# Linear-attention kernel on one core: the order of work in the entry, on four engines

## The reference

```python
xn = _layernorm(x)
def layer(h, p):                        # 8 layers, scan
    q = elu(h @ wq + bq) + 1; k = elu(h @ wk + bk) + 1; v = h @ wv + bv
    kv = einsum('bshd,bshm->bhdm', k, v)
    z = 1 / (einsum('bshd,bhd->bsh', q, k.sum(axis=1)) + 1e-6)
    att = einsum('bshd,bhdm,bsh->bshm', q, kv, z)
    h = _ln(h + att @ wo + bo, g1, be1)
    y = gelu(h @ w1 + c1) @ w2 + c2
    return _ln(h + y, g2, be2)
s = _ln(layers(_ln(xn)), gf, bef)       # x -> xn -> layers
g = silu(expert_ffn(xn))                # one expert of 8 for each sequence
out = x + s * g
```

## Time and profile before

| | |
|---|---|
| median of 3 runs | 856.59 us (856.33 to 857.17) |
| the profiled execution's own time | 854.89 us |
| its span, first to last instruction | 853.2 us |
| what lies around the span | 1.69 us |
| busy share of PE, DVE, ACT, POOL | 95%, 90%, 86%, 48% |
| the entry, until the first FFN matmul starts | 41.78 us |
| granted clock of TensorE, mean | 0.981 of 2.4 GHz |

### The profile page before, as it was taken

How to read it: one execution, slowest core, us unless ns; L and a number is a source line. 1 busy time by engine, 2 the same in 40 slices (tenths; PEclk the granted TensorE clock), 3 DMA queues, 4 the chain that set the end, 5 groups by cost and what they waited for, 6 DMA issues and landing times.

```text
span 853.2 us, 19244 instructions
## 1 busy us (share of the span) xinstructions
PE 809.6 (95%) x5914; PEld 734.4 (86%) x5914; DVE 766.1 (90%) x2672; ACT 736.2 (86%) x1315; POOL 411.1 (48%) x393
## 2 busy tenths in 40 slices
PE   5698999999999999999999999999999999999885
PEld 4588899999999999999999999999999999988652
DVE  6988999989899899999899899999999898999865
ACT  2589999989998899989998899988999899988764
POOL 5234445445544454445444544445453544465656
PEclk9899999999999999999999999999999999999985
DMA  5300100000010100101010100101010000000001
GB/s 149 90 2 2 44 2 19 17 16 30 2 35 2 44 2 5 31 11 35 1 36 2 45 1 1 35 2 44 2 35 2 2 2 1 7 21 1 1 27 74
DMA packets 26264, 18.76 MB, mean 22 GB/s; under 512 B 4354, under 2 KB 22195, under 8 KB 26164
## 3 DMA queue, kind: packets, MB, share of 16 engines
q1 hardware_dynamic: 25300, 16.95, 7.2%
q10 hardware_dynamic: 864, 0.59, 0.3%
HBM read 15.43 MB, written 2.10 MB: 21 GB/s over the span
## 4 chain that ended last, share of the span: by engine, by line
PE 79%; DVE 10%; ACT 6%; issue 3%; POOL 2%; DMA 0%; POOLq 0%; ACTq 0%; DVEq 0%
PE down_ps L762 21%; PE att_ps L723 6%; PE small_ps L693 6%; PE up_ps L752 5%; PE up_ps L754 5%; PE up_ps L753 5%; PE t_ps L671 4%; PE t_ps L730 4%; PE kq_ps L683 3%; PE kq_ps L684 3%; PE kq_ps L685 3%; DVE z_lo L1042 2%; ACT z_hi L913 2%; PE up_ps L714 2%; PE small_ps L701 2%
## 5 line engine op out<-in xcount | busy, mean ns | idle before, releaser
L762 PE MATMUL down_ps<-w_use,hid 128*128 128x128 f32 x2048 | 259.7, 275 | 0.2 <-ACT hid L864 0.2
L762 PEld LDWEIGHTS down_ps<-w_use,hid 128*128 128x128 f32 x2048 | 243.9, 192 | 2.1 <-ACT hid L864 1.2
L1060 POOL TENSOR_TENSOR res_ffn<-z_tm,g_ffn 128x512 f32<-128x512 f32 x64 | 81.8, 1278 | 241.6 <-DVE k_e L1173 235.8
L1049 POOL TENSOR_TENSOR res_att<-z_tm,g_att 128x512 f32<-128x512 f32 x64 | 82.5, 1289 | 153.1 <-DVE h L1000 153.1
L864 ACT ACTIVATE hid<-up_ps 128x512 f32<-128x512 f32 x192 | 113.6, 593 | 23.0 <-PE up_ps L754 15.6
L1012 DVE BATCH_NORM_STATS2 st<-h 128x6 f32<-128x128 f32 x504 | 107.4, 276 | 0.1
L919 ACT ACTIVATE z_tm<-h,shift,rstd 128x128 f32<-128x128 f32 x248 | 101.5, 483 | 1.9 <-DVE shift L1029 1.9
L752 PE MATMUL up_ps<-z_hi,w_hi 128*128 128x512 f32 x192 | 86.3, 449 | 1.7 <-ACT hid L864 1.7
L1063 POOL TENSOR_TENSOR res_ffn<-res_ffn,ffn_row 128x512 f32<-128x512 f32 x64 | 84.1, 1314 | 5.0
L1052 POOL TENSOR_TENSOR res_att<-res_att,att_row 128x512 f32<-128x512 f32 x64 | 82.4, 1287 | 5.0
L683 PE MATMUL kq_ps<-w_kq_hi,zq_hi 128*128 128x256 f32 x256 | 81.8, 320 | 1.5 <-DVE zq_lo L956 1.5
(11 more groups left out here) (225 smaller groups left out, 1969.1 us busy)
## 6 DMA issues: line engine op xcount, KB each, us to landing
raw_w<-in_L_attn_W SPq DMA_DIRECT2D x15, 256.0 KB, 4.3
out_y<-gate_tm SPq DMA_DIRECT2D x8, 256.0 KB, 2.1
bias_bc<-in_L_attn_c SPq DMA_DIRECT2D x7, 256.0 KB, 4.3
x_tm<-in_L_attn_x SPq DMA_DIRECT2D x3, 512.0 KB, 7.9
raw_rows<-in_L_attn_be SPq DMA_DIRECT2D x15, 64.0 KB, 4.1
raw_g<-in_L_attn_g SPq DMA_DIRECT2D x14, 64.0 KB, 3.3
x_tm<-in_L_attn_x SPq DMA_DIRECT2D x2, 256.0 KB, 3.4
raw_rows<-in_L_attn_bo SPq DMA_DIRECT2D x8, 64.0 KB, 3.8
```

The source lines that it names most:

```text
L762: last = nc.tensor.matmul(down_ps[:, t, :], hid[:, j, t * P:(t + 1) * P], w2_use[:, j, :], start=(j == 0), stop=(j == FC - 1))
```

## The change

Four streams are reordered. No instruction's size changes, and none is added or removed. Four instructions (`xz` of sequence 1) change engine from VectorE to ScalarE.

- VectorE: the statistics of group 3 move from behind `rden` of unit 0 to directly behind those of group 2, ahead of the first `k_e`. `dve_shift_x(1)` moves ahead of the copies of the first attention weights.
- ScalarE: `act_xz(1)` is put ahead of the first keys, and `act_rstd_x(3)` moves from the end of period 0 to the end of the period before it.
- TensorE: `pe_fold_w1_first` moves out of period 0 to behind it, that is behind `pe_att` of unit 0.
- GpSimd: the residual of unit 0 now waits for `tk` (the first `k_e`), and that of unit 1 waits for the three affine instructions and stands ahead of `pool_ffn_rows` and `pool_w2`.

```diff
 # gpsimd
+                pool.wait_ge(s["tk"], 1)
                 pool_period(pool, 0, 0)
+                pool.wait_ge(s["aff_s"], 3)
+                pool_period(pool, 0, 1)
                 pool_ffn_rows(pool, 0, False)
                 pool.wait_ge(s["raw_w20"], 16)
                 pool_w2(pool, 0, False)
-                pool_period(pool, 0, 1)
-                pool.wait_ge(s["t2m"], 2)
+                pool.wait_ge(s["gffn_ready"], 2)
+                pool.wait_ge(s["w2_ready"], 1)
 # tensor
-                pe_period(pe, 0, 0, lambda: pe_fold_w1_first(pe))
+                pe_period(pe, 0, 0)
+                pe_fold_w1_first(pe)
 # scalar
-                act_period(act, -1, SEQS - 1, None, lambda: act_rstd_x(act, 2))
-                act_period(act, 0, 0, lambda: act_rstd_x(act, 3), lambda: act_xz(act, 2))
+                act_xz(act, 1)
+                act_period(act, -1, SEQS - 1, lambda: act_rstd_x(act, 3), lambda: act_rstd_x(act, 2))
+                act_period(act, 0, 0, None, lambda: act_xz(act, 2))
 # vector
+                dve_shift_x(dve, 1)
                 dve_fold_att_first(dve)
                 dve_state_lo(dve, 0)
-                dve_shift_x(dve, 1)
-                dve_xz(dve, 1)
                 dve_stats(dve, 2)
+                dve_stats(dve, 3)
                 dve_period(dve, -1, SEQS - 1)
-                dve_period(dve, 0, 0, None, statistics_3, first_affines)
+                dve_period(dve, 0, 0, None, None, first_affines)
```

More of the change, by code:

```diff
@@ L1597, in first_affines @@
                     dve_shift_x(dve, 2)
-                def statistics_3():
-                    dve_stats(dve, 3)
-                dve_period(dve, 0, 0, None, statistics_3, first_affines)
+                dve_period(dve, 0, 0, None, None, first_affines)
                 dve_period(dve, 0, 1, None, lambda: dve_split_w1_first(dve), lambda: dve_shift_x(dve, 3))
```

## The result

The changed kernel is slower. Over 11 executions each, its median is 860.89 us (854.94 to 862.32), and that of the kernel before is 856.33 us (854.42 to 857.98); the ratio is 1.0048, with a 95% interval of 1.0033 to 1.0062. That is 4.1 us (2.8 to 5.3). (The quotient of the two medians, 1.0053, isn't the ratio, but lies in its interval; the text goes by the ratios.) The forecast was 857.3 with a range that ended at 859.3. The change also widened the spread of the executions, from 3.6 to 7.4 us. The profiled execution took 859.23 us, with a span of 857.5 (before 854.89 and 853.2).

A forecast was written before the change was run, and what follows sets the result against it. The prediction took a chain of waits, mostly on VectorE, before the first FFN matmul (41.78 us) as the bound. Its terms, -1.11 + 2.00 - 0.15 = +0.74 us, gave 856.6 + 0.7 = 857.3 us, range 855.3 to 859.3.

The forecast's parts named there:

- The order: Predicted chain: ScalarE's q_n, attention of unit 0, fold, keys of unit 1, then g_sb, for which VectorE waits some 2.2 us.
- the fold's bare price of 2.00: On TensorE between attention of unit 0 and keys of unit 1: the moved fold adds 2.00 us ahead of g_sb.
- The hand-over of the norm to the end: Time gained or lost at g_sb of unit 1 passes to the norm and the program's end, one for one.
- the clock's part: TensorE's clock stays full from kvo of unit 0 to the attention, and is half from the norm's transposes, as before.
- 1.3 us of work in 4: TensorE's predicted work between the end of kvo of unit 0 (about 23) and the attention (27).
- the prediction's own sign of being wrong: A granted TensorE clock of 0.5 between 24 and 31 us would show the forecast wrong.
- The second rival: TensorE's clock falls in the new idle time, slowing attention of unit 0 and fold: +2.2 to +3.4 us, chance 0.19.
- The gain of 1.11 us ahead of the fold: ScalarE's q_n no longer waits for VectorE's q_nt, so attention of unit 0 starts at 26.96 instead of 28.07.
- The statistics ahead of the first keys: On VectorE, group 3's statistics cost 2.3 us, paid by 1.0 of idle time and 0.9 of contention; k_phi 0.31 late.
- the 1.1 that ScalarE's list was to let through: Of the 2.4 us that VectorE gave at q_nt, only 1.11 reaches the attention of unit 0, behind ScalarE's work.
- The small terms: Minor effects, among them mr_x of group 3 on VectorE taking 0.15 instead of 0.29 us: 0.15 gained.
- Contention on `k_e`: With GpSimd held back, VectorE's first k_e takes 0.41 us instead of 1.32.

The follow-up runs named there:

- e12: e8 with the first FFN fold again behind the attention of unit 0 and e3's five unread matmuls in period 0; 853.94 us, 0.9985 of the kernel before.
- e11: The kernel before plus e8's unread matmuls, two ahead of the first keys and four ahead of the norm's transposes; 855.57 us, ratio 1.0007.
- e3: The changed kernel plus five unread matmuls in TensorE's idle time of period 0; 856.49 us, 1.0007 of the kernel before.
- e5: The changed kernel run again without any edit; 861.31 us, 1.0060 of the kernel before.
- e6: The changed kernel plus four unread matmuls ahead of the norm's transposes; 856.05 us, 1.0018 of the kernel before.
- e2: The kernel before with only the first FFN fold moved behind the attention of unit 0; 857.90 us, ratio 1.0026.
- e4: The changed kernel with the statistics of group 3 and their ScalarE part in their old place; 858.11 us, 1.0036 of the kernel before.
- e1: The changed kernel with the first FFN fold back in its old place; 854.24 us, 0.9982 of the kernel before.
- e7: e1 with GpSimd's residual of unit 1 gated on shift_x of sequence 2 instead of the affines; 854.21 us, 0.9991 of the kernel before.
- e8: e7 plus unread matmuls, two ahead of the first keys and four ahead of the norm's transposes; 852.30 us, 0.9971 of the kernel before.
- e9: e1 with the statistics of group 3 back in their old place; 856.68 us, 1.0017 of the kernel before.
- e10: The kernel before with only the two GpSimd gates and the new GpSimd order; 856.77 us, ratio 1.0017.

## Why the prediction was wrong

**The order was right.** The fold went into the path, `g_sb` of unit 1 is what VectorE waits for, ScalarE's `q_n` follows `q_e` without a wait (it stands behind it at 27.37), and the fold's bare price of 2.00 is 2.1 us in the path and 1.2 to 1.6 us in the time (e12). The hand-over of the norm to the end, taken as one for one, holds to within 1.7 us over all profiles; between these two the 3.39 us of `g_sb` became 3.25 at the norm's transposes, 2.78 at the first FFN matmul and 4.34 in the time.

**The step that failed is the clock's part.** The prediction said "I take it as kept" of the idle time between TensorE's `kvo` of unit 0 and its attention, on the evidence of one row with 1.10 us of work in 3.37 at full clock. (Its 1.3 us of work in 4 is an error of addition: 1.10 and the 0.49 of the product with `w_o` are 1.6, and 1.68 were measured from 24 to 28.) In the changed kernel's profile that same stretch ended at half clock, with the attention at 2.07 and the first fold matmuls at 1.50, and so the prediction's own sign of being wrong, a granted clock of 0.5 between 24 and 31, was there. The row was a single execution; in e11 the same stretch with the same work ended at half clock.

At `g_sb` of unit 1 the forecast had 31.05, and 33.55 was measured. Of these 2.50 us, 1.46 lie between the start of the attention and `g_sb`, which took 5.55 us instead of 4.09 because attention and fold ran in part at half clock. The other 1.04 are the gain ahead of it, which didn't come (next but one paragraph). The same piece took 4.19 and 4.20 with fillers (e3, e12), 4.79 in e5 and 7.83 in e6, where the clock stayed low through the keys too. The second rival had named this mechanism, its place and a price (+2.2 to +3.4, measured +4.1) and got a chance of 0.19. It left the keys of unit 1 at full clock. As e3 shows, it was the main effect.

The rule of the Trainium skill that was weighed there (TensorE: Matmul & The Clock Gate, "HAM oscillation"), that bursts separated by waits are throttled and start at half rate, holds in this profile: 2.07 against 1.16 us for the same eight attention passes. It doesn't decide each case. Over the fourteen profiles, the attention of unit 0 was at half clock, wholly or for the most part, in all five with the fold behind it and no fillers (the changed kernel, e2, e4, e5, e6), and at full clock in both with fillers in that idle time (e3, e12). With the fold in its old place it was at full clock in four (before, e1, e7, e8) and at half in three (e9, e10, e11). So the fold in the idle time makes the full clock possible and doesn't ensure it.

**The gain of 1.11 us ahead of the fold.** This is a second term that was mis-sized by the clock. The attention started at 28.00 instead of the forecast 26.96, so in this pair of profiles nothing was left of it. The prediction let the projections of unit 1 reach full clock at 21.85 as they had the earlier trace rows, behind keys of unit 0 at full clock. Here these keys took 2.09 for 1.16 and the projections ran wholly at half clock, so ScalarE's `k_e` of unit 1 came at 23.53 and not at 22.5. With ScalarE's list in the path, as the change has it, that goes straight to the attention. It was the same in e1, e3, e6 and e7 (keys 2.07 to 2.08, attention at 27.76 to 28.02). The gain exists where the clock is better: the attention started at 26.61 in e5 and at 25.64 in e8.

**The statistics ahead of the first keys.** The prediction made `k_phi` 0.31 late. It started at 16.44, where it was 16.52 before. The DMA of sequences 2 and 3 landed about a us earlier in this execution (statistics at 11.79 for 12.77), and `k_phi` then waited 0.56 for ScalarE's `q_e`. So the price was zero here, in part by the luck of that landing. The value, 3.0 us by e1 against e9, was far above the 1.1 that ScalarE's list was to let through.

**The small terms.** Contention on `k_e` (1.32 to 0.43) and on the affines went as computed. GpSimd's start was put 0.16 behind the affines and was 0.08, so it got in ahead of `shift_x`, which cost 1.1 and, by e7, nothing in the time. `mr_x` of group 3 took 0.15 at 34.53.

**What stays open.** Why the gates alone are slower (e10); why the fold's move costs 2.2 us in the old order (e2) and 5.7 in the new one; what decides between full and half clock when the work is the same (before and e11); and how the 3.5 us divide between the attention, the fold, the keys and the norm over many executions, since there is one trace for each kernel, and two for the changed one.

## What to carry to other kernels

Ahead of the steady part, an instruction moved out of an idle time can cost twice: its duration where it lands, and the clock that it helped to keep up where it was. Here that was 5.7 us in one order and 2.2 in the other, for 2.0 us of matmuls. Before a matmul is moved, look for whose idle time it filled, and price the next matmuls at both levels of the clock. And when one profile shows full clock beyond an idle time, ask how many executions it speaks for: a spread of the times of several us (3.6 in the kernel before) is a sign that it may not speak for all.

## What the runs showed of the hardware

- The same matmuls take 1.8 to 1.9 times as long on TensorE where the clock stands at half: attention, fold and keys took 7.83 us in e6 and 4.79 in e5. Matmuls that nobody reads, put in an idle time, took 3.5 us off the changed kernel (e3) and narrowed its spread to a third. In the kernel before they gained nothing (e11).
- A tiny instruction can last as long as a large one beside it. `shift_x` started 0.03 us behind GpSimd's residual (20.89 and 20.86, 1.27 us) and ended 0.03 behind it: 1.27 for 0.17. In e7, where GpSimd starts behind it, it took 0.17. It goes the other way too: in e7 GpSimd's copy L307 took 0.75 us beside VectorE's `q_nt` and ended 0.15 behind it; in the changed kernel the same copy took 0.29.
- `q_nt` took 1.06 us in e7, beside a GpSimd residual (22.27 to 23.58), and 0.66 undisturbed. It isn't of the `tensor_scalar` kind: it reads `q_elu` and `rden`, both in SBUF. The Trainium skill (GPSIMD Engine Reference, "8. Key points") says that VectorE's instructions with two SBUF inputs contend with GpSimd as well as those in a two-port mode. The traces agree.
- In e2 the four `xz` of sequence 1 on VectorE took 3.17 us beside GpSimd's first residual, which started at 11.57 in that execution; in the profile of before it started at 13.59, and they were over at 12.57. In e11 they met in the same way (3.26 us). The changed kernel has them on ScalarE and cannot meet this:

```profile
11.44 3.17 DVE L396 TENSOR_SCALAR z_tm<-x_tm,r_x,shift_x 128x128 f32<-128x128 f32 x4
```
